# Attention on one core: low parts and residual add moved to GpSimd, statistics in four pieces

## The reference, cut to what matters

```
x = x + attention(layernorm(x), w_in, b_in, w_out, b_out)
qkv = x @ w_in.T + b_in              # 16 heads of 8 features each
scores = einsum('bhqd,bhkd->bhqk', q * 8**-0.5, k) + causal mask
out = softmax(scores) @ v            # back to [tokens, 128]
out = out @ w_out.T + b_out
out = where(isnan(out), 0, out)
```

## Time and profile before

| | before |
|---|---|
| median of 3 runs | 1771.24 us (1767.77 to 1772.6) |
| the profiled execution | 1770.8 us |
| its span, first to last instruction | 1767.8 us |
| TensorE matmul busy over the span | 1632.6 us (92%) |
| VectorE / ScalarE / GpSimd busy | 1287.2 / 1016.6 / 775.2 us |
| the attention stage | about 218 to 836 us of the span |
| in it: PE / DVE / ACT / POOL busy | 561.65 / 468.13 / 356.26 / 127.01 us |
| mean granted TensorE clock | 0.976 of full speed |

### The profile page before, as it was taken

The page is one execution under the profiler, slowest core; times in us unless marked ns, Lnnn a source line. Parts: engine busy times, 40 slices in busy tenths (PEclk is TensorE's granted clock), DMA queues, the critical chain, the costliest instruction groups (busy, mean ns, idle before and its releaser), DMA issues. The chain is left out here.

```text
span 1767.8 us, 25916 instructions
## 1 busy us (share of the span) xinstructions
PE 1632.6 (92%) x8360; PEld 1159.7 (66%) x8360; DVE 1287.2 (73%) x3879; ACT 1016.6 (58%) x1718; POOL 775.2 (44%) x734
## 2 busy tenths in 40 slices
PE   5999889899899999997999989999998988999998
PEld 3777546555555555554777767777777876777776
DVE  6777578788778878862888767677666876777775
ACT  4666416565665666565666656555555645555554
POOL 2666601312311311121566656555573524555555
PEclk9999959999999999998999999999999998999999
DMA  4332121111111111100333341111110002111120
GB/s 149 98 98 94 54 36 33 20 23 23 25 30 21 26 21 34 20 11 14 109 118 121 103 135 55 48 49 48 55 43 1 1 2 94 56 55 60 55 95 19
DMA packets 58247, 95.01 MB, mean 54 GB/s; under 512 B 9313, under 2 KB 17121, under 8 KB 58113
## 3 DMA queue, kind: packets, MB, share of 16 engines
q1 hardware_dynamic: 56000, 91.07, 18.1%
q10 hardware_dynamic: 2112, 2.30, 0.4%
HBM read 76.76 MB, written 2.88 MB: 45 GB/s over the span
## 5 line engine op out<-in xcount | busy, mean ns | idle before, releaser
L697 DVE TENSOR_TENSOR big<-banks,big 128x512 f32<-128x512 f32 x384 | 264.6, 689 | 202.2 <-ACT banks L634 160.3
L1159 ACT ACTIVATE big<-banks 128x1024 f32<-128x1024 f32 (+3 forms) x384 | 301.5, 811 | 174.7 <-PE banks L1070 169.2
L634 ACT ACTIVATE banks<-banks 128x512 f32<-128x512 f32 x384 | 224.0, 583 | 276.5 <-PE banks L577 271.3
L707 DVE TENSOR_TENSOR big<-big,banks 128x512 f32<-128x512 f32 x400 | 274.9, 687 | 29.7 <-PE banks L580 15.8
L1051 PE MATMUL banks<-arena 128*128 128x512 f32 (+3 forms) x768 | 250.6, 403 | 27.5 <-DVE att_mx L1284 15.2
L1199 POOL TENSOR_SCALAR_AFFINE_SELECT big<-big 128x512 f32<-128x512 f32 x128 | 81.2, 635 | 403.7 <-ACT big L1159 403.7
L1284 DVE CUSTOM_DVE_ANT_0 banks<-banks,att_mask 128x128 f32<-128x128 f32 (+3 forms) x512 | 234.0, 523 | 29.2 <-PE banks L1051 28.5
L667 POOL TENSOR_TENSOR ffn1b_hid_l<-big,ffn1b_hid_h 128x512 fp32r<-128x512 f32 x128 | 165.4, 1292 | 128.6 <-ACT ffn1b_hid_h L639 128.6
L1070 PE MATMUL banks<-arena 128*128 128x512 f32 (+3 forms) x768 | 207.4, 356 | 12.0 <-ACT big L1159 12.0
L667 POOL TENSOR_TENSOR ffn1a_hid_l<-big,ffn1a_hid_h 128x512 fp32r<-128x512 f32 x128 | 165.3, 1292 | 116.6 <-ACT ffn1a_hid_h L639 116.6
L577 PE MATMUL banks<-xh,arena 128*128 128x512 f32 x512 | 208.0, 406 | 8.2 <-PEq L1450 6.8
(11 more groups left out here) (256 smaller groups left out, 3171.6 us busy)
## 6 DMA issues: line engine op xcount, KB each, us to landing
big<-weight_rows SPq DMA_DIRECT2D x256, 128.0 KB, 2.9
big<-weight_rows SPq DMA_DIRECT2D x128, 256.0 KB, 4.1
arena<-att_parts SPq DMA_DIRECT2D x16, 384.0 KB
arena<-att_parts SPq DMA_DIRECT2D x128, 48.0 KB
w_raw<-in_ffn_w_dram SPq DMA_DIRECT2D x12, 256.0 KB, 3.0
out_dram<-x SPq DMA_DIRECT2D x8, 256.0 KB, 2.3
setup_raw<-in_ffn_w_dram SPq DMA_DIRECT2D x3, 576.0 KB, 7.1
gau_angle<-in_consts_dram SPq DMA_DIRECT2D x2, 512.0 KB, 7.3
```

What stands on the lines that cost most here:

```text
L634: act.activation(gate if c < NSCALED else sil, gate, ACT.Silu).then_inc(silu_done, 1)
L697: dve.tensor_tensor(scl[:, num % 2, :], gate_ps[:, num % NB, :], share[:, c // PER, :], ALU.mult)\
L707: dve.tensor_tensor(hid[:, num % NH, :], scl[:, num % 2, :] if c < NSCALED else sil, up_ps[:, num % NB, :], ALU.mult).then_inc(hidden, 1)
L1159: act.activation(probs[:, unit % NPROB, 2 * pair:2 * pair + 2, 0:c], score_ps[:, pair, :, 0:c], ACT.Exp, scale=SCALE).then_inc(exped, 1)
```

## The change

1. **Queries and keys.** ScalarE reads the bank twice: once rounded into the high part, once in full fp32 into a scratch half of `xn` (`whole(h)`), and the second read frees the bank. GpSimd subtracts to get the low part and then makes the second copy of the high part. VectorE has no `proj` entry any more. For w = 1 ScalarE first waits until GpSimd has finished w = 0 of the same half, because both use the same scratch; `qk_again` now also says that the low part is there.
2. **Output projection.** For batches 0 to 2 VectorE only adds the bias; GpSimd takes max(y, 0), adds it to `x`, takes min(y, 0), adds that. For batch 3 VectorE does all three steps itself, straight into `x`, and GpSimd nothing.
3. **Statistics.** The eight `bn_stats` are four entries of two, 0.04 of a section apart, and the aggregation is an entry of its own.

```diff
-                    put(n - 2.6, "stats", b)
+                    for q in range(NB // 2):
+                        put(n - 2.64 + 0.04 * q, "stats", b, q)
+                    put(n - 2.46, "aggr", b)
...
+        def whole(h):
+            return xn[:, h * TG:(h + 1) * TG, :].rearrange("p t d -> p (t d)")
...
             def proj(b, w, h):                                  # ScalarE
-                bank, _ = content(act, "proj", b, w, h)
+                bank, empty = content(act, "proj", b, w, h)
...
-                act.activation(parts[:, w, 0, cut], bank, ACT.Identity, bias=b_in[:, w:w + 1]).then_inc(qk_high, 1)
+                if w == 0:
+                    drained(act, "ln", b, h)
+                else:
+                    act.wait_ge(qk_again, 4 * b + h + 1)
+                act.activation(parts[:, w, 0, cut], bank, ACT.Identity, bias=b_in[:, w:w + 1])
+                act.activation(whole(h), bank, ACT.Identity, bias=b_in[:, w:w + 1]).then_inc(empty, 1)
...
             def proj(b, w, h):                                  # GpSimd
-                step = 4 * b + 2 * w + h
                 cut = slice(h * G, (h + 1) * G)
-                pool.wait_ge(qk_high, step + 1)
+                drained(pool, "proj", b, w, h)
+                pool.tensor_tensor(parts[:, w, LOW[w], cut], whole(h), parts[:, w, 0, cut].bitcast(F32), ALU.subtract)
                 pool.tensor_copy(parts[:, w, AGAIN[w], cut], parts[:, w, 0, cut].bitcast(F32)).then_inc(qk_again, 1)
...
             def wo(b, h):                                       # GpSimd
+                if b == B - 1:
+                    return
...
-                pool.wait_ge(y_steps, 2 * step + 2)
-                pool.tensor_tensor(xs, xs, ypos[:].rearrange("p t d -> p (t d)"), ALU.add).then_inc(x_added, 1)
+                drained(pool, "wo", b, h)
+                drained(pool, "ln", b + 1, HALF - 1)
+                above = xn[:, h * TG:(h + 1) * TG, :].rearrange("p t d -> p (t d)")
+                pool.tensor_scalar(above, y[:, h, :], 0.0, None, ALU.max).then_inc(x_added, 1)
+                pool.wait_ge(x_added, 4 * step + 1)
+                pool.tensor_tensor(xs, xs, above, ALU.add).then_inc(x_added, 1)
+                pool.tensor_scalar(y[:, h, :], y[:, h, :], 0.0, None, ALU.min).then_inc(x_added, 1)
+                pool.wait_ge(x_added, 4 * step + 3)
+                pool.tensor_tensor(xs, xs, y[:, h, :], ALU.add).then_inc(x_added, 1)
...
-            def proj(b, w, h):                                  # VectorE, gone
-                bank, empty = content(dve, "proj", b, w, h)
-                cut = slice(h * G, (h + 1) * G)
-                dve.wait_ge(qk_high, 4 * b + 2 * w + h + 1)
-                dve.scalar_tensor_tensor(parts[:, w, LOW[w], cut], bank, b_in[:, w:w + 1], parts[:, w, 0, cut].bitcast(F32),
-                                         ALU.add, ALU.subtract).then_inc(empty, 1)
...
             def wo(b, h):                                       # VectorE
...
+                if b == B - 1:
+                    xs = k.x[:, b * S + h * G:b * S + (h + 1) * G]
+                    drained(dve, "wo", b, h)
+                    dve.scalar_tensor_tensor(xs, y[:, h, :], 0.0, xs, ALU.max, ALU.add).then_inc(y_steps, 1)
+                    dve.wait_ge(y_steps, h + 1)
+                    dve.scalar_tensor_tensor(xs, y[:, h, :], 0.0, xs, ALU.min, ALU.add)
```

More of the change, by code:

```diff
@@ L962, in phase_attention @@
         on_t = v_t
-        y, ypos = sb("y", [P, TG, D]), sb("ypos", [P, TG, D])
+        y = sb("y", [P, HALF, G])
         score_ps = k.banks[:, 0:4, :].rearrange("p (n h) c -> p n h c", h=2)
@@ L971, in phase_attention @@
         moments, eps_done, rstd_done, norm_done = begun.moments, begun.eps_done, begun.rstd_done, begun.norm_done
-        xh_done, qk_high, qk_again = sem("xh_done"), sem("qk_high"), sem("qk_again")
+        xh_done, qk_again = sem("xh_done"), sem("qk_again")
         neg_steps, max_in = sem("neg_steps"), sem("max_in")
@@ L1247, in _, with stats, aggr @@
         def _(dve):
[L1248 to L1251, removed]
+            def stats(b, q):
+                for t in range(2 * q, 2 * q + 2):
                     ins = dve.bn_stats(st[:, t, :], k.x[:, b * S + t * P:b * S + (t + 1) * P])
-                ins.then_inc(moments, 1)
+                if 2 * q + 2 == NB:
+                    ins.then_inc(moments, 1)
+            def aggr(b):
+                dve.wait_ge(norm_done, b)
                 dve.wait_ge(moments, 2 * b + 1)
@@ L1317, in wo @@
                 step = b * HALF + h
-                dve.tensor_tensor(y[:], bank.rearrange("p (t d) -> p t d", d=D),
+                if b > 0:
+                    dve.wait_ge(x_added, 4 * (step - HALF) + 4)
+                dve.tensor_tensor(y[:, h, :].rearrange("p (t d) -> p t d", d=D), bank.rearrange("p (t d) -> p t d", d=D),
                                   bo[:].unsqueeze(1).broadcast_to([P, TG, D]), ALU.add).then_inc(empty, 1)
[L1320 to L1328, removed]
+                if b == B - 1:
[4 more added lines that the diff above has]
+                    dve.scalar_tensor_tensor(xs, y[:, h, :], 0.0, xs, ALU.min, ALU.add)
+            walk(dict(stats=stats, aggr=aggr, ln=ln, max=peak, neg=neg, ot=ot, wo=wo), lead.vector(dve, bank=4 + LENT))
 class SplitAhead:
```

## The result

The changed kernel takes **1755.39 us** (median of 7 runs, 1754.5 to 1760.0) against 1769.01 us for the kernel before in 7 runs beside it; the ratio is 0.9936 (95% interval 0.9922 to 0.995), so it is faster by 0.64%. Set on the median of 1771.24 us that was shown beforehand, the ratio gives 1759.9 us. Its profiled execution took 1760.0 us, 10.8 us less than the one before, with a span of 1756.7 us, 11.1 us less.

What follows compares the result with a forecast made beforehand. TensorE leads a plain section (busy 30.72 of 31.69 us), but VectorE's gapless masked maxima move its end nearly one for one. Terms -2.0 - 3.9 - 2.4 + 3.3 - 1.5 = -6.5 us from 1770.8 gave 1764.3 us, range 1757 to 1772.

Steps and rivals of the forecast that it cites:

- term 1: Statistics in pieces, three sections: only the clock drop is saved, nothing for the spreading as such; -2.0 us.
- term 3: Queries and keys, batches 1 to 3: shorter ring bank holds and maxima sooner; 3 x -0.8 = -2.4 us.
- term 2: Output projection, batches 0 to 2: VectorE loses two instructions per half; 3 x -1.3 = -3.9 us.
- rival B: Statistics: the pieces find holes, 6.9 us more gained, 1757.4 us; chance 0.11.
- rival A: Output projection and projections: VectorE's relief is not on the path, both gains 0, 1770.6 us; chance 0.20.
- D: Projections: ScalarE's second reads hold up the exponentials, 3 x +2.6 us there, 1774.5 us in all; chance 0.08.
- Term 4: Projection, batch 0: GpSimd's three entries in a row delay the first keys; +3.3 us.
- Term 5: Output projection, batch 3, at the stage's end: six VectorE instructions, 4.3 us instead of 5.8; -1.5 us.
- C: Output projection: GpSimd's max and min slow at 3.18 us each, masks late, 1776.3 us; chance 0.05.

Runs made afterwards that it cites:

- wo_only: The kernel before with only the change to the output projection; 1763.25 us, ratio 0.9978 to the kernel before.
- vector_load_kept: The changed kernel with an unused VectorE reduction put back at each projection place of batches 1 to 3, without its hold on the bank; 1763.34 us, single run.
- pieces_aggr_at_once: The changed kernel with the aggregation directly behind the fourth statistics piece instead of two banks later; 1763.8 us, ratio 0.9975 to the kernel before.
- max_thrice: The changed kernel with two more unused GpSimd maxima per half of each output projection of batches 0 to 2; 1773.64 us, one run.

## Why the prediction was right, and where not

Faster by more than 0.3% was forecast with 0.56, and so it came out. The profiled execution took 1760.0 us against the 1764.3 predicted, and the ratio set on the median shown gives 1759.9, inside the range of 1757 to 1772; the bare median of 1755.39 lies 1.6 us below its lower end. The direction was right and the sum too small: the 6.5 us forecast are a ratio of 0.9963, outside the interval measured. Of the 4.3 us missing in the profiled execution, 3.1 are term 1; term 3 and the last window add 1.4 and 1.3, term 2 and the first window take 0.5 and 0.7 back. That the time still lies inside the range is in part luck: the range reached that low for rival B, which had a chance of 0.11, and part of B's size came by another cause.

- **Term 1** (-2.0) was right on the clock: it stayed at 1.00 in all three sections, and the stall went. It failed on the sentence "So I take nothing for the spreading as such", and on the claim that "the aggregation two banks later" stands in the same gapless stretch and is "paid in full". VectorE's stretch is gapless, but what it costs is decided by TensorE: with the aggregation two banks on, the value product covers the delay. Measured: 1.0 us more for each of three sections, by the aggregation's place alone. Equal waits with and without statistics showed that this one place had no hole, not that the stretch has none; rival B, which read the pieces as the possible gain, had part of the size (6.9 us forecast beyond the clock, 3.1 measured) but named the pieces.
- **Term 2** (-3.9) came to -3.4. The relief is on the path, and rival A falls: wo_only alone shortens just these sections by 0.8 to 1.1 us.
- **Term 3** (-2.4) came to -3.8, of which 0.3 us is a shorter DMA wait in the first. Both causes I gave are in the rows. The shorter holds bring 0.9 us a section where the working had 0.5, "some 0.2 us less per hold" being nearer 0.3: this is the part that was sized too small. The maxima that no longer queue behind ScalarE's result bring 0.3, as forecast. VectorE's own load is worth nothing, as vector_load_kept shows. D falls: ScalarE's busy time rose from 25.91 to 28 us without a cost.
- **Term 4** (+3.3) hit the first window's start to 0.1 us, by a piece of luck: 2.5 of it arose in this stage, and 0.8 had come from the stage before. The path was as told: GpSimd's third entry ends at 232.86, and the keys' DMAs go out at 232.94, 3.6 us later than before.
- **Term 5** (-1.5) came to -1.6 between the last bias add and the last write of `x`. The other 1.2 us of the last window belong to its clock, 0.96 against 0.90, which varies from run to run with no edit.
- **C**, GpSimd's maximum and minimum: "I take 0.62, because copy and mask have the same columns and one input" was wrong, 1.49 measured, and the chain took 11.35 us for 8.0. That it cost nothing is due to the room: the value product would have begun to wait from some (2.46 / 4) + 1.49 = 2.1 us per instruction, near the 2.2 given, though I had counted with the second mask where the first decides. The Trainium skill (GPSIMD Engine Reference, Engine selection) has one-input operations roughly at line rate: the copy at 0.611 us comes near that, the maximum and minimum at 1.49 us do not: the same maximum took VectorE 0.43 us before the change (L1323), and they are slower even than the two-input add at 1.28.

## What to carry to other kernels

When work has to stand in one engine's gapless stretch, do not price it by its own duration: look at what the engine that waits for it does next, and put the work where the waiting engine has something that needs none of its results. A moved read of a shared buffer is worth what it takes off the hold of the buffer, which TensorE's waits tell, and what it brings forward of the drains queued behind it, and not what it takes off the engine that did it. And where an operation's price is unknown, the distance to the next thing in its queue that is waited for is the number that decides; find out which one that is.

## What the runs showed of the hardware that was not expected

- GpSimd's maximum or minimum of 128 x 512 fp32 with a constant took 1.49 us, against 0.43 on VectorE, and on GpSimd 0.61 for a copy, 0.635 for the causal mask and 1.28 for an add or subtraction of two tiles.
- TensorE's clock, at 0.50 of full in short stretches, was cut in statistics sections after stalls of 0.96 us (pieces_aggr_at_once, one of three) to 2.3 us (7 of 9 with the old order, all behind the same stall of 2.25 to 2.27 us), and in none of 25 whose longest stall was 0.56 us or less. In max_thrice, with stalls of some 3.25 us, all three affected sections show it. Whether the length of the stall decides was not tried by itself.
